# Merge shares of a step's two work lists: TensorE's and VectorE's time of each item together, in place of one engine's time per list

## What is computed

```python
x = x + 0.5 * ffn(layernorm(x))     # 32 experts of 96, top 6, and a shared one of 192
x = x + attn(layernorm(x))          # h = h + mamba(rmsnorm(h)); h = h + mlp(rmsnorm(h))
x = x + 0.5 * ffn(layernorm(x))     # the same weights as above

# ffn: all experts for all tokens, combined by the routing weights
g = einsum('td,edf->tef', x, wg); u = einsum('td,edf->tef', x, wu)
routed = einsum('tef,efd,te->td', silu(g) * u, wd, combine)
# mamba, per step of the sequence
hstate = exp(dt * A) * hstate + (dt * x) * B
y = einsum('bhgn,bhn->bhg', hstate, C)
```

## Time and profile before

| | |
|---|---|
| three runs | 1778.46, 1781.56, 1782.30 us, median 1781.56 |
| profiled execution | 1783.27 us, of which 1781.4 are the span of its instructions |
| PE matmul busy | 1551.8 us, 87% of the span |
| PE weight load busy | 1165.3 us, 65% |
| DVE busy | 1265.5 us, 71% |
| ACT, POOL busy | 843.5 us (47%), 988.8 us (56%) |
| DMA | 113 GB/s over the span |
| mean granted clock of PE | 0.958 |

### The profile page before, as it was taken

How to read it: one execution, slowest core, us unless ns; L and a number is a source line. 1 busy time by engine, 2 the same in 40 slices (tenths; PEclk the granted TensorE clock), 3 DMA queues, 4 the chain that set the end, 5 groups by cost and what they waited for, 6 DMA issues and landing times. The chain is left out here.

```text
span 1781.4 us, 22496 instructions
## 1 busy us (share of the span) xinstructions
PE 1551.8 (87%) x7088; PEld 1165.3 (65%) x7088; DVE 1265.5 (71%) x2067; ACT 843.5 (47%) x1692; POOL 988.8 (56%) x1048
## 2 busy tenths in 40 slices
PE   5998887887899889888998799879987998889979
PEld 4665554546566567666776677667765776667868
DVE  4553587876868788968797879778977787777321
ACT  4443454543555346535553466346634564444323
POOL 1663354654767457636665566447644666458525
PEclk9999999999999999999999999999998999889989
DMA  4565221123323232423232333233322333233434
GB/s 161 205 217 192 75 95 50 63 77 103 133 90 113 97 121 92 138 88 116 95 126 96 98 115 128 89 104 116 126 95 73 124 114 113 80 112 131 133 100 149
DMA packets 73430, 202.35 MB, mean 114 GB/s; under 512 B 10049, under 2 KB 22561, under 8 KB 72929
## 3 DMA queue, kind: packets, MB, share of 16 engines
q1 hardware_dynamic: 65120, 175.75, 29.6%
q0 software_dynamic: 8192, 25.17, 4.6%
HBM read 175.46 MB, written 25.43 MB: 113 GB/s over the span
## 5 line engine op out<-in xcount | busy, mean ns | idle before, releaser
L1478 POOL TENSOR_TENSOR ring<-ring 128x512 f32<-128x512 f32 x192 | 256.9, 1338 | 378.9 <-DVE ring L1358 378.6
L808 PE MATMUL gub<-x_hi,wr 128*128 128x384 f32 (+2 forms) x1040 | 428.9, 412 | 29.1 <-DVE hid L1175 22.4
L889 PE MATMUL acc<-hid,w_down 128*128 128x384 f32 (+2 forms) x1040 | 408.1, 516 | 15.6 <-POOL hid L1457 15.5
L1457 POOL TENSOR_TENSOR hid<-hid,u_sb 128x384 f32<-128x384 f32 (+2 forms) x260 | 292.0, 1123 | 182.2 <-ACT u_sb L1041 168.0
L810 PE MATMUL gub<-x_hi,wr 128*128 128x384 f32 (+2 forms) x1040 | 370.0, 356 | 0.0
L809 PE MATMUL gub<-x_lo,wr 128*128 128x384 f32 (+2 forms) x1040 | 369.8, 356 | 0.0
L1352 DVE TENSOR_TENSOR_SCAN ring<-decays,side 128x512 f32<-128x512 f32 x256 | 310.4, 1213 | 40.1 <-ACT decays L1139 37.3
L1051 ACT ACTIVATE hid<-gub 128x384 f32<-128x384 f32 (+2 forms) x324 | 156.6, 483 | 365.9 <-PE gub L850 189.5
L1041 ACT ACTIVATE u_sb<-gub 128x384 f32<-128x384 f32 (+2 forms) x260 | 132.2, 508 | 336.6 <-PE gub L810 336.5
L1465 POOL TENSOR_TENSOR hid<-hid,weight 128x384 f32<-128x384 f32 (+2 forms) x240 | 267.6, 1116 | 29.6 <-ACT weight L1031 15.0
L889 PEld LDWEIGHTS acc<-hid,w_down 128*128 128x128 f32 x1040 | 185.7, 192 | 110.9 <-issue 41.8
(11 more groups left out here) (117 smaller groups left out, 1856.8 us busy)
## 6 DMA issues: line engine op xcount, KB each, us to landing
wr<-w_halves SPq DMA_DIRECT2D x234, 512.0 KB, 3.3
wm_gu<-in_w_mlp POOLq DMA_DIRECT2D x64, 256.0 KB, 3.1
w_halves<-wr SPq DMA_DIRECT2D x26, 512.0 KB, 3.2
wm_down<-in_w_mlp POOLq DMA_DIRECT2D x64, 128.0 KB, 2.7
w_raw<-in_w_gu SPq DMA_DIRECT2D x26, 256.0 KB, 3.7
rows<-parts SPq DMA_DIRECT2D x16, 384.0 KB, 2.3
cst<-rows SPq DMA_DIRECT2D x48, 128.0 KB, 2.5
xin<-in_x SPq DMA_DIRECT2D x8, 256.0 KB, 3.0
```

The lines of the kernel that those rows point to most:

```text
L808: mm(out, w[:, 0, half, k, :], x_hi[:, k, a:b], start=(k == 0), stop=False)
L889: last = mm(acc[k][:, a:b], w, h[:, a:b], start=(c == 0), stop=(c == (MLP_CHUNKS if mlp else FFN_CHUNKS) - 1))
L1457: nc.gpsimd.tensor_tensor(h, h, u_sb[c % USLOTS][:, a:b], ALU.mult).then_inc(sem["hidden"], 1)
L1478: add(ysum, ysum, ring[:, ring_at(it)], ALU.add).then_inc(sem["y_sum"], 1)
```

## The change

Nearly all entries of `WEIGHT` get new numbers, and `merge` looks an item up by its first two parts too, so that ("down", "mlp") can have another length than the `down` of the experts. `SPACE`, the passes after the merge and all instructions stay as they are: every step holds the same items in another order. Steps -1 and 9 are not merged and stay the same.

```diff
-WEIGHT = {"n1": 0.5, "nc": 0.7, "n2": 0.5, "nm": 1, "rq": 0.75, "split": 0.5, "sr": 0.9, "sl": 0.9, "x": 0.5, "xc": 1.6, "xd": 1.6,
...
-          "ub": 2, "unit": 2, "rt1": 1, "yz": 0.4, "outp": 0.5, "om": 1.6,
-          "g": 1.3, "u": 1.3, "down": 1.7, "gum": 1.7, "cmb": 0.2,
+WEIGHT = {"ub": 0.9, "unit": 2.1, "x": 1.7, "split": 1.7, "z": 1.7, "dt": 0.9, "n1": 0.9, "n2": 0.9, "outp": 3.5,
...
+          "g": 1.2, "u": 1.2, "by_g": 0.6, "down": 1.5, "cmb": 0.2, "gum": 2.5, ("down", "mlp"): 0.9, "end": 1.6,
...
-            at += length.get(it, length.get(it[0], 0.1))
+            at += length.get(it, length.get(it[:2], length.get(it[0], 0.1)))
```

More of the change, by code:

```diff
@@ L321, in items_of @@
     return out
-WEIGHT = {"n1": 0.5, "nc": 0.7, "n2": 0.5, "nm": 1, "rq": 0.75, "split": 0.5, "sr": 0.9, "sl": 0.9, "x": 0.5, "xc": 1.6, "xd": 1.6,
-          "xm": 0.7, "z": 0.5, "zm": 0.7, "dt": 0.5, "sp": 1.6, "sp_dt": 1.6, "sp_x": 0.9, "y0": 0.6,
-          "ub": 2, "unit": 2, "rt1": 1, "yz": 0.4, "outp": 0.5, "om": 1.6,
-          "g": 1.3, "u": 1.3, "down": 1.7, "gum": 1.7, "cmb": 0.2,
+WEIGHT = {"ub": 0.9, "unit": 2.1, "x": 1.7, "split": 1.7, "z": 1.7, "dt": 0.9, "n1": 0.9, "n2": 0.9, "outp": 3.5,
+          "rt1": 0.9, "xc": 1.9, "xd": 1.9, "xm": 0.9, "zm": 0.7, "sr": 0.7, "sl": 1.0, "sp": 1.6, "sp_dt": 2.2,
+          "sp_x": 1.0, "nc": 0.7, "nm": 0.9, "om": 1.4, "yz": 0.8, "rq": 0.75, "y0": 0.1,
+          ("n1", "rms1"): 0.1, ("n1", "rms2"): 0.1,
+          "g": 1.2, "u": 1.2, "by_g": 0.6, "down": 1.5, "cmb": 0.2, "gum": 2.5, ("down", "mlp"): 0.9, "end": 1.6,
           **{(k, w): x for w in ("lnO", "rmsO") for k, x in (("n1", 2), ("nc", 2), ("n2", 3), ("nm", 2))},
```

## The result

The changed kernel took 1818.49 us (median of 4 runs, 1814.71 to 1819.34), the kernel before 1780.01 in the same series. The ratio is 1.0214, with a 95% interval of 1.0192 to 1.0235. The forecast was 1772 and faster, and its range ended at 1788.

The account below looks back on a forecast made before the run. Neither PE nor DVE bounds a whole step; in-order stalls of 1 to 3 us lose time. -8.4 - 3.0 + 5.6 - 2.5 - 1.4 = -9.7 from 1783.3 gives 1773.6; the median 1.7 lower, 1772; range 1757 to 1788.

Parts of the forecast that it names:

- term C: Tails of steps 1 to 7: DVE gets `ub 1` later, PE's stall at `ub 2` grows 0.8 us each, +5.6 us.
- the end of a step gives nothing back: Step ends: said because the last `down` already waits 2.86 us for POOL.
- Rival R2: Tails: all 2.4 us of `ub 1` delay stays and slow rows follow, 28 us lost, 1794 us; chance 0.18.
- forecast's own sign of being wrong: Whole kernel: PE's busy time growing by more than 3 us at unchanged instructions would make the prediction wrong.
- A: MLP part of steps 3, 5 and 6: filled stalls outweigh a new wait for `gum 6`, -8.4 us.
- rival R1: Gaps only move: `side` banks set the pace, new waits at `ub 9`, `dt`, `gum 6`; 1781.6 us; chance 0.19.
- B: Steps 2 and 4: `down` fills the stall at `rt1`, DVE's wait for `unit 14` goes, -3.0 us.
- D: Step 1: `u 12` and `g 13` fill the 4.35 us stall at `ub 12`, -2.5 us; `ub 0` counted 0.
- E: Steps 7 and 8: `end mlp` goes ahead of a scan, so `n1` waits less, net -1.4 us.
- the DMAs: Transfers that move with their items: counted as 0; without cover one would cost up to 3.3 us.

Follow-up runs that it names:

- g4: Kernel before, with `unit 5` put behind `down 23` in steps 3, 5 and 7 also: 1764.31 us, ratio 0.9917.
- e3: Changed kernel, with the last four items of steps 2, 4 and 6 as before (`unit 5` behind `by_u 25`): 1803.80 us, 1.0131.
- g2: Kernel before, with only the last four items of steps 2, 4 and 6 new (`unit 5` ahead of `by_u 25`): 1801.91 us, 1.0115.
- f1: Kernel before, with the new order only in the MLP part of steps 2 to 6: 1789.18 us, 1.0046.
- f3: Kernel before, with the new order only from the MLP part's end to `outp` in steps 3, 5 and 6: 1781.09 us, 0.9993.
- h1: Kernel before, with the new order only in the MLP part of steps 3, 5 and 6: 1790.03 us, 1.0041.
- h2: Kernel before, with the new order only in the MLP part of steps 2 and 4: 1783.53 us, 1.0007.
- f2: Kernel before, with the new order only in step 1 up to its `outp`: 1782.86 us, 1.0006.
- f4: Kernel before, with the new order only in step 7 up to its `outp`: 1794.14 us, 1.0072.
- g1: Changed kernel, with the tails of steps 1 to 7 and the pair `down 4`, `unit 9` in steps 7 and 8 as before: 1792.53 us, 1.0060.
- g3: Kernel before, with the new order only in step 7 from `by_g 3` to `outp`: 1785.17 us, 1.0028.
- h3: Kernel before, with the new order only from `outp` to `down 21` in steps 1 to 7: 1794.63 us, 1.0071.
- e2: Kernel before, with the new order only behind `outp` in steps 1 to 7: 1811.71 us, 1.0182.
- e4: Changed kernel, with the stretch from `outp` to `down 21` in steps 1 to 7 as before: 1810.14 us, 1.0165.
- e1: Changed kernel, with the order of before from `outp` on in steps 1 to 7: 1796.24 us, 1.0085.

## Why the prediction was wrong

**The end of a step was not followed.** This is the step that failed first. In term C, I traced the moved items up to `ub 2` and stopped. The last items of steps 2, 4 and 6 moved too, and my sum put that at nothing without a reason. Behind it stands the sentence "the end of a step gives nothing back": I read the 2.86 us wait of the last `down` for POOL in the earlier trace rows as a floor, when it was a wait that the order makes, which can grow (1.58 to 4.83 us in step 4) and shrink (2.86 to 1.13 us in step 3 of g4). By e3 and g2 this is worth 15 to 21 us, the largest piece. Rival R2 had the place, the tail, but not this wait: its 28 us were worked out at `ub 1` and `ub 2`, and with it the time would have been 1794. The forecast's own sign of being wrong was there as well: PE's busy time grew by 8.0 us, and the limit was 3. And by steps, where I had 3, 5 and 6 shorter by 2 us each, all of steps 2 to 7 became longer, by 1.6 to 9.9 us.

**C was right in kind and too small.** I had worked it out on step 3 and taken it seven times. In step 3 it came out: DVE's wait at `ub 1` was to be near 4 us and PE's stall at `ub 2` 2.3, and the kernel after has

```profile
765.02 0.70 DVE L1342 TENSOR_TENSOR side<-dtx,side 128x512 f32<-128x512 f32 x1 [3.98 <-PE side L985]
...
769.36 0.39 PE L985 MATMUL side<-bst,sel_b 96*128 96x256 bf16 x2 [1.99 <-DVE res L1373]
```

Step 5 is the same. But the stall at `ub 2` grew from 0.74 to 4.28 us in step 1, from 1.50 to 3.15 in step 2 and from 2.01 to 3.34 in step 4, and not at all in steps 6 and 7. The price of 0.8 us a step was too small: the stretch costs 8.4 to 12.9 us in all, against 5.6. What I left to rival R2 happens in part: in steps 1 and 2 the rows behind the longer stall ran at the lower level of the clock, where they had not before. Step 2, the 4.3 us from `ub 2` on, before and after:

```profile
584.79:589.09 4.30, 4.29 (x18) 2.76 (x19) 2.96 (x4) 0.60 (x1) 2.61 (x3) 1.00 0.00 0
583.43:587.73 4.30, 4.30 (x14) 3.42 (x14) 1.92 (x2) 0.60 (x1) 1.14 (x2) 0.62 0.02 8
```

In step 4 this is hardly new: the granted clock there is 0.50 behind the stall of 3.34 us, and was 0.60 behind that of 2.01. The 2.4 us do not all stay, as R2 had it: from `om` to `by_g 25`, steps 3 and 5 get 2.1 us back.

**A failed at the word "go".** The stall at `ub 7` and DVE's wait for `gum 5` did go, and the wait for `gum 6` came out at 2.42 us where I had 1.9. But I counted only DVE's waits. PE's new ones at `dt` and `ub 9`, which rival R1 had named, take the rest, and the balance in step 3 of f1 is zero. The 2.30 us for `by_g 0` went too, in f3 and in the kernel after, and f3 has no gain from it: PE stalls 4.31 us at one `g` there, where two such stalls made 2.1 us before. The Trainium skill, in Perfetto Trace Analysis, section Optimization Strategy, says that a repeating gap can mean a lack of buffers, and the trace of f1 agrees: each new stall of PE there is for a `side` bank.

That A costs 7 to 8 us instead of nothing comes from steps 3, 5 and 6 (h1), and the clock at `dt` goes with it. Seven kernels have the new MLP order in steps 3 and 5, which gives fourteen stretches from the scan of `unit 6` to that of `unit 16`. In three of them `dt` took 1.10 us at a granted clock of 1.00, and the stretch 52.8 to 53.2 us, as before. In the other eleven `dt` took 1.33 to 2.05 us at 0.50 to 0.78, and the stretch 54.1 to 57.6. In the ten kernels with the old order there `dt` took 1.03 us at 1.00 every time, and the stretch 50.9 to 54.4. So the new order puts `dt` where the clock is often low. That this is all of A's cost was not tested.

**B, D.** In B, DVE's wait at the read-out behind `rt1` did go (h2, step 4), but the gain of 3 us is not there (h2, 1.0007, at most 0.07% faster). D failed at the place itself: `ub 12` of step 1 still waits, and step 1 gains nothing (f2).

```profile
263.70 0.61 PE L985 MATMUL side<-bst,sel_b 96*128 96x256 bf16 x2 [4.24 <-DVE ring L1354]
```

The stall kept its 4.35 us of the earlier trace rows less 0.11. I had not counted what left the place: `u 12` and `g 13` came in front of `ub 12`, but `down 9`, 1.88 us, moved away from there, and on DVE `by_g 12`, 0.68 us, now stands ahead of the scan that frees the bank. Counted from the same row of the routing on DVE, PE reaches the stall 0.8 us later than before, and the scan ends 0.7 us later.

**E and the DMAs.** `n1` in step 7 waits 0.63 us for the residual, as forecast (below 1.5). But the row ahead of it had waited 3.21 for the load:

```profile
1383.42 1.10 PE L891 MATMUL acc<-hid,wm_down 128*128 128x256 f32 x4 [3.21 <-DMA wm_down<-in_w_mlp]
...
1385.37 2.03 PE L908 MATMUL side<-x,mean_w 128*128 128x256 f32 x4 [0.63 <-DVE x L1207]
```

"Apart from D no moved transfer is one that a stall names" was true of the kernel before and the wrong question. `md 7` kept its place in the list and was passed by `unit 9`, on POOL alone. Step 7 costs 12 us (f4), of which the load is some 3, by the 2.7 us at `by_g 0` that g1 takes back, and the order of the chunks alone 4 (g3). The remaining 5 arise in the chunks too, but only when the part ahead of them is new as well; they were not taken apart. Step 8 with the new order was not run by itself.

**What stays open.** The pieces add to more than the whole: about 15 to 21 (`unit 5`), 8 to 13 (C), 7 to 8 (A) and 12 (step 7) against 38 measured. Within the tail they do add up: 21 (g2) and 13 (h3) against 30 (e2), and taken back 14.7 (e3) and 8.4 (e4) against 22 (e1). The tail and the part ahead of it do not: 30 (e2) and 14 (e1) against 38. What they share I did not separate further.

## What to carry over

When an order changes, ask of each moved item what stands behind it on every queue, and do so to the very end of the stage: here the largest loss was a wait of an item that closes a step. Work that nobody needs yet belongs behind the work that closes a stage: one such item in three steps cost 21 us when it was put ahead (g2), and gave 17 us when it was put behind (g4), each more than any term of the forecast. And a stall that is filled is gained only if the waits of both engines, counted together over the stretch, become shorter; in f1 and f3 they did not. A term worked out in one step is to be looked up in each step that it is taken for.

## What the runs showed of the chip

Some of DVE's rows became longer without any change in their work. In step 3 of the kernel after, DVE and POOL:

```profile
646.34 1.50 DVE L1365 TENSOR_TENSOR yg<-xs,z 128x256 f32<-128x256 f32 x1
652.40 2.38 DVE L1327 TENSOR_TENSOR dtx<-dtx,lbuf 128x512 f32<-128x512 f32 x1
...
645.90 1.65 POOL L1480 TENSOR_TENSOR ring<-ring 128x512 f32<-128x512 f32 x1 [5.12 <-DVE ring L1360]
...
651.96 1.31 POOL L1480 TENSOR_TENSOR ring<-ring 128x512 f32<-128x512 f32 x1
```

In step 3 of the kernel before, the same two rows took 0.42 and 0.82 us; at other places of that kernel nearly half of the rows of `yg` took over 1 us as well. Both read two tiles that lie in SBUF, and both began here, in the kernel after, while POOL was in the middle of a row; the first ended 0.3 us after POOL's did. Over the run these two lines cost DVE 6.7 and 6.4 us more, which is more than its 9.2 in all. The Trainium skill, in Perfetto Trace Analysis, section Optimizing Scalar/DVE Operations, says that GpSimd and DVE share an SBUF read port; these rows agree with it, but no run here took POOL's row away to prove it. How much of the 38 us this makes was not measured. It need not be much: in the trace of f3 the `dtx` line took 5.1 us more than in the kernel before and the `yg` line 1.7, and f3 was as fast (0.9993).
